# Splitting the LayerNorm and token-mix work of a transformer layer into pairs of chunks between attention steps

## The reference

```python
q = einsum('bsm,hmd->bhsd', x, kernel[0]); k = ... kernel[1]; v = ... kernel[2]
attn = softmax(einsum('bhsd,bhtd->bhst', q, k) / (d * d * h))
out  = einsum('bhst,bhtd->bhsd', attn, v) -> (b, s, d*h);  out = out @ WO[0]
y = layernorm(x + out)
y_prev = y shifted by one token, zero at the start
xr = mu_r * y + (1 - mu_r) * y_prev;  xk = mu_k * y + (1 - mu_k) * y_prev
r = sigmoid(xr @ W_r.T);  k_act = relu(xk @ W_k.T) ** 2
result = layernorm(y + r * (k_act @ W_v.T))
```

## Time and profile before

| what | value |
|---|---|
| median of 3 runs | 2945.0 us (2942.08 to 2955.33) |
| profiled execution | 2821.61 us, span of the slowest core (core 3) 2819.8 us |
| spans of the 8 cores | 2805.7 to 2819.8 us |
| granted TensorE clock, mean | 0.877 to 0.882 |
| TensorE matmul busy | 2124.7 us (75%) |
| ScalarE busy | 1247.8 us (44%) |
| VectorE busy | 835.2 us (30%) |

### The profile page before, as it was taken

How to read it: one execution, slowest core, us unless ns; L and a number is a source line. 1 busy time by engine, 2 the same in 40 slices (tenths; PEclk the granted TensorE clock), 3 DMA queues, 4 the chain that set the end, 5 groups by cost and what they waited for, 6 DMA issues and landing times.

```text
span 2819.8 us, 30056 instructions; the slowest of 8 cores (2805.7 to 2819.8 us)
## 1 busy us (share of the span) xinstructions
PE 2124.7 (75%) x10176; PEld 713.3 (25%) x10176; DVE 835.2 (30%) x1369; ACT 1247.8 (44%) x1441; POOL 20.1 (1%) x27
## 2 busy tenths in 40 slices
PE   0037888778977897789677978887888788878845
PEld 0013322222322232223223322222322222222212
DVE  0012200240434043404362205042233323332365
ACT  0000178357445754574400364646554655365611
POOL 0000000000000000000000000000000000000000
PEclk9998988878988898889888999888988898889867
DMA  9961300000320032002301103000130013001201
GB/s 174 209 169 30 90 1 1 30 1 13 93 90 1 9 96 90 1 4 87 105 15 30 60 30 108 28 30 1 60 105 30 1 60 105 31 1 60 90 30 60
DMA packets 85135, 157.23 MB, mean 56 GB/s; under 512 B 1984, under 2 KB 16384, under 8 KB 84992
## 3 DMA queue, kind: packets, MB, share of 16 engines
q1 hardware_dynamic: 61968, 123.84, 13.5%
q0 software_dynamic: 23024, 31.47, 7.4%
HBM read 155.31 MB, written 31.46 MB: 66 GB/s over the span
## 4 chain that ended last, share of the span: by engine, by line
PE 54%; ACT 18%; DVE 12%; DMA 9%; issue 7%; ACTq 1%; DVEq 0%; POOL 0%; SPq 0%; POOLq 0%
PE psg L99 27%; ACT pb L109 12%; PE pspv L99 10%; PE psden L99 10%; ACT lta L109 4%; DMA ws<-wts 3%; PE psa L99 3%; PE psb L99 3%; DMA wsc<-ws 2%; DVE xka L118 2%; DMA aba<-xT 2%; DVE stv L118 2%; DVE recb L118 2%; DVE xra L118 2%; DVE y L118 2%
## 5 line engine op out<-in xcount | busy, mean ns | idle before, releaser
L109 ACT ACTIVATE pb<-psa 128x1024 bf16<-128x1024 f32 x512 | 522.8, 1021 | 424.5 <-PE psa L99 423.4
L109 ACT ACTIVATE pb<-psb 128x1024 bf16<-128x1024 f32 x512 | 523.8, 1023 | 406.9 <-PE psden L99 230.6
L99 PE MATMUL pspv<-pb,vtb 128*64 128x512 bf16 x2048 | 433.3, 431 | 59.8 <-DVE aba L118 59.7
L99 PE MATMUL psden<-pb,cstb 128*32 128x512 bf16 x2048 | 416.1, 415 | 0.0
L99 PE MATMUL psg<-xra,ws 128*128 128x512 bf16 x1320 | 353.7, 421 | 0.6 <-DVE xra L118 0.6
L99 PE MATMUL psg<-aba,ws 128*128 128x512 bf16 x632 | 164.4, 417 | 241.9 <-DMA ws<-wsc 188.9
L99 PE MATMUL psa<-qtb,ktb 64*128 64x512 bf16 x1024 | 214.2, 409 | 148.6 <-ACT pb L109 88.8
L118 DVE TENSOR_TENSOR aba<-pspv,rsb 128x512 bf16<-128x512 f32 x64 | 44.3, 691 | 814.6 <-ACT rsb L109 814.6
L99 PE MATMUL psb<-qtb,ktb 64*128 64x512 bf16 x1024 | 212.8, 403 | 61.1 <-ACT pb L109 61.1
L99 PEld LDWEIGHTS pspv<-pb,vtb 128*64 128x64 bf16 x2048 | 111.1, 109 | 328.3 <-issue 328.2
L99 PEld LDWEIGHTS psg<-xra,ws 128*128 128x128 bf16 x1320 | 128.3, 105 | 202.2 <-issue 97.2
(11 more groups left out here) (100 smaller groups left out, 1595.0 us busy)
## 6 DMA issues: line engine op xcount, KB each, us to landing
ws<-wsc SPq DMA_DIRECT2D x36, 2048.0 KB, 9.4
ws<-wts POOLq DMA_DIRECT2D x8, 2048.0 KB, 25.3
y<-xT SPq DMA_DIRECT2D x8, 2048.0 KB, 10.4
outT<-outb SPq DMA_DIRECT2D x32, 512.0 KB, 3.5
wsc<-ws SPq DMA_DIRECT2D x7, 2048.0 KB, 13.0
aba<-xT POOLq DMA_DIRECT2D x8, 1024.0 KB, 8.9
xra<-xT POOLq DMA_DIRECT2D x6, 1024.0 KB, 10.0
cstf<-cst SPq DMA_DIRECT2D x1, 96.0 KB, 2.4
```

The lines of the kernel that those rows point to most:

```text
L99: i = e.matmul(_o, _l, _r, start=_st, stop=_sp, tile_position=_tp, skip_group_check=True)
L109: i = e.activation(_o, _i, _f, scale=_s, bias=_b)
```

## The change

The function that broadcasts and applies a LayerNorm is cut into a head (the two `psg<-sr` matmuls and the two activations) and four pieces of one pair of chunks each; the mix is cut into four pieces of one pair each. In the six tiles with `t` > 0 the head becomes a filler of step 19, and application and mix pieces alternate at steps 21, 23, 25, ... 35. LayerNorm 2 of the tile before is cut in the same way: head and four pieces are fillers of their own (due for `t` > 0 at steps 100, 102, ... 108; for `t` = 0 at 75, 77, ... 83). Where a function calls the pieces in a row (the key/value stage and the tail), the order stays as it was.

```diff
-            def emit_ln_bcast_apply(u, dst_y1):
-                Ybuf = OUTB
+            def emit_ln_bcast_head(u, dst_y1):
                 b1 = next_bank()
                 wait("t", c_va, u["nsr"])
...
+            def emit_ln_apply_pair(st, op):
+                if op == 0:
+                    wait("v", c_g, st["nmean"])
+                    wait("v", c_ar, st["nrs"])
+                wait("v", c_va, c_va.n)
...
+                if op == 6:
+                    st["b0b"].free = (c_va, nap)
+                    last_nap[0] = nap
...
+            def emit_mix_pair(u, op):
+                wait("v", c_va, c_va.n)
...
-                        def u_bcast(p=prev):
-                            emit_ln_bcast_apply(p, Y1)[0]
-                            emit_mix(p)
+                        lnst = {}
+                        def u_bhead(p=prev, s=lnst):
+                            s["st"] = emit_ln_bcast_head(p, Y1)
+                        def mk_ap(op, s=lnst):
+                            return lambda: emit_ln_apply_pair(s["st"], op)
+                        def mk_mx(op, p=prev):
+                            return lambda: emit_mix_pair(p, op)
                         fillers.append((17, u_stats))
-                        fillers.append((21, u_bcast))
-                        steps = [50 + 3 * i for i in range(18)]
+                        fillers.append((19, u_bhead))
+                        for i, op in enumerate(range(0, 8, 2)):
+                            fillers.append((21 + 4 * i, mk_ap(op)))
+                            fillers.append((23 + 4 * i, mk_mx(op)))
+                        steps = [50 + 3 * i for i in range(17)]
+                        steps += [100 + 2 * i for i in range(5)]
                     else:
-                        steps = [24 + 3 * i for i in range(18)]
+                        steps = [24 + 3 * i for i in range(17)]
+                        steps += [75 + 2 * i for i in range(5)]
```

More of the change, by code:

```diff
@@ L502, in emit_ln_bcast_apply @@
                 b1.free = (c_ar, nrs)
-                wait("v", c_g, nmean)
-                wait("v", c_ar, nrs)
-                nap = 0
-                naps = []
-                for op in range(0, 8, 2):
[L508 to L524, removed]
@@ L525, in emit_ln_bcast_apply @@
-                b0b.free = (c_va, nap)
-                last_nap[0] = nap
-                return nap, naps
+                return {"b0b": b0b, "nrs": nrs, "nmean": nmean, "naps": [],
+                        "dst": dst_y1}
+            def emit_ln_apply_pair(st, op):
+                Ybuf = OUTB
+                dst_y1 = st["dst"]
+                if op == 0:
+                    wait("v", c_g, st["nmean"])
+                    wait("v", c_ar, st["nrs"])
+                wait("v", c_va, c_va.n)
+                for j, scr in ((op, STV), (op + 1, RECB)):
+                    np1 = vop("scalar_tensor_tensor",
+                              (scr[:, :], st["b0b"].ap[:, :], -1.0,
+                               Ybuf[:, j * QT:(j + 1) * QT],
+                               ALU.mult, ALU.add),
+                              inc=(c_va if j == op + 1 else None))
+                wait("v", c_va, np1)
+                nap = 0
+                for j, scr in ((op, STV), (op + 1, RECB)):
+                    dst = (dst_y1[:, j * 516 + 4: j * 516 + 4 + QT]
+                           if dst_y1 is not None
+                           else Ybuf[:, j * QT:(j + 1) * QT])
+                    nap = vop("tensor_tensor",
+                              (dst, scr[:, :], LTA[:, 512:1024], ALU.mult),
+                              inc=c_va)
+                st["naps"].append(nap)
+                if op == 6:
+                    st["b0b"].free = (c_va, nap)
+                    last_nap[0] = nap
+                return nap
@@ new lines, in emit_ln_bcast_apply @@
+            def emit_ln_bcast_apply(u, dst_y1):
+                st = emit_ln_bcast_head(u, dst_y1)
+                for op in range(0, 8, 2):
+                    emit_ln_apply_pair(st, op)
+                return st["naps"][-1], st["naps"]
+            def emit_mix_pair(u, op):
+                wait("v", c_va, c_va.n)
+                for j, scr in ((op, STV), (op + 1, RECB)):
+                    nd = vop("tensor_tensor",
+                             (scr[:, :], Y1[:, j * 516 + 4: j * 516 + 4 + QT],
+                              Y1[:, j * 516 + 3: j * 516 + 3 + QT],
+                              ALU.subtract),
+                             inc=(c_va if j == op + 1 else None))
+                wait("v", c_va, nd)
+                for j, scr in ((op, STV), (op + 1, RECB)):
+                    vop("scalar_tensor_tensor",
+                        (XRA[:, j * QT:(j + 1) * QT], scr[:, :],
+                         MUS[:, j:j + 1],
+                         Y1[:, j * 516 + 3: j * 516 + 3 + QT],
+                         ALU.mult, ALU.add))
+                for j, scr in ((op, STV), (op + 1, RECB)):
+                    nk = vop("scalar_tensor_tensor",
+                             (XKA[:, j * QT:(j + 1) * QT], scr[:, :],
+                              MUS[:, 8 + j:9 + j],
+                              Y1[:, j * 516 + 3: j * 516 + 3 + QT],
+                              ALU.mult, ALU.add),
+                             inc=(c_va if j == op + 1 else None))
+                wait("v", c_va, nk)
+                if op == 6:
+                    u["mix_done"] = vop(
+                        "tensor_copy",
+                        (bass.AP(Y1, 3, [[NCH * 516, 128], [516, 8], [1, 1]]),
+                         bass.AP(Y1, 515, [[NCH * 516, 128], [516, 8], [1, 1]])),
+                        inc=c_va)
@@ L529, in emit_mix @@
             def emit_mix(u):
-                wait("v", c_va, c_va.n)
                 for op in range(0, 8, 2):
[L532 to L557, removed]
+                    emit_mix_pair(u, op)
             def make_fillers(u, load_wo=True):
@@ L687, in ln2_stats, with ln2_head, ln2_pair, f @@
                     u["nsr"] = nsr
-                def ln2_bcast():
-                    nap, naps = emit_ln_bcast_apply(u, None)
-                    u["naps"] = naps
+                ln2s = {}
+                def ln2_head():
+                    ln2s["st"] = emit_ln_bcast_head(u, None)
+                def ln2_pair(op):
+                    def f():
+                        emit_ln_apply_pair(ln2s["st"], op)
+                        if op == 6:
+                            u["naps"] = ln2s["st"]["naps"]
+                    return f
                 for oc in range(8):
@@ L699, in make_fillers @@
                 fl.append(ln2_stats)
-                fl.append(ln2_bcast)
+                fl.append(ln2_head)
+                for op in range(0, 8, 2):
+                    fl.append(ln2_pair(op))
                 return fl
```

## The result

| | median of runs | undisturbed runs |
|---|---|---|
| changed kernel | 2766.31 us (8 runs) | 2763.74 to 2768.46 |
| kernel before: the three first runs and five timed beside the changed kernel | 2857.57 us (8 runs) | 2817.49 to 2824.43 |

The ratio is 0.9807, with a 95% interval of 0.9794 to 0.9821: on 2821 us, 54.4 us (50.5 to 58.1). I had forecast 54 us. The time forecast, 2891 us with a range of 2866 to 2914, is nevertheless wrong by 125 us, because I took the 54 from 2945. Of either kernel some executions run with a lower TensorE clock on the cores of one die or both and are some per cent longer (one of the changed kernel took 2903.57 us); the others are called undisturbed here. The three runs shown ahead of the prediction (2942 to 2955) are the longest on record of the unchanged kernel, whose undisturbed executions later took 2817 to 2842.

A forecast was written before the change was run, and what follows sets the result against it. TensorE's value matmuls waited 63.4 us for VectorE's multiply, queued behind LayerNorm and mix. Six tiles x (7.1 + 1.7) plus 0.75 gave 54 us off the 2945.0 median: 2891 us, range 2866 to 2914.

The forecast's parts named there:

- the base: Runs' median of 2945.0 us, 123 above the profiled execution; the same 54 us taken off, giving 2891 us.
- First term: Head 1's multiply, six tiles: three pairs' application and mix ahead instead of four, 21.1 us against 28.2; 7.1 us a tile.
- Second term: Statistics matmuls directly behind head 0's epilogue matmul: VectorE starts 1.7 us earlier a tile, ends 0.5 and 3.0.
- What is late next: At head 1, VectorE still last: multiply at +28.1 instead of +36.9, a shorter stop of 2 to 5 us left.
- First rival: Filled hole behind head 0's epilogue keeps clock high: 11 to 13.4 us a tile, 66 to 80, 2872 us; chance 0.17.
- Its second condition: Shorter stop at head 1 shortens low clock behind it from 5 us to 1 or 2, saving 1 to 3 us.
- Second rival: Low-clock stretch around head 1's stop keeps 15 us: 5.2 us a tile left, 2914 us; chance 0.12.
- Slower: Clock does not come back for heads 0 and 1: 9.7 us a tile worse, 3003 us; chance 0.04.
- Edits at nothing: Fourth pair behind multiply, mean's held bank and extra waits cost nothing; the waits bounded by 1 us a tile.

The follow-up runs named there:

- the order alone: Changed kernel with statistics back at step 21, pairs' application and mix given together, three before head 1's multiply, one behind; ratio 0.9837 to the kernel before.
- the version with two pairs: Changed kernel with two pairs' application and mix before head 1's multiply and two behind, instead of three and one; ratio 0.9661 to the kernel before, span 2733.6 us.

## Why the prediction was right in its sum and wrong in its time

**The step that failed: the base.** I wrote that the 123 us between the three runs shown and the profiled execution "is not in the trace", and took the gain from the runs' median. The profiled execution, 2821.61 us, was an undisturbed one. It lies within the 2817.49 to 2824.43 of the undisturbed runs timed beside the changed kernel. From it the forecast is 2768 us, against 2766.31 measured. What made the three first runs 123 us longer stays open, since the clocks of their cores were not recorded. I had both numbers and no evidence for either as the base; a range that covered both bases would have begun near 2740. I gave the base no rival and no chance of its own, though it was more than twice as large as the gain.

**First term, 7.1 us a tile: right.** A pair takes 7.13 us, and the order alone gave 46 us (26 to 65) against 43; the spans differ by 43.

**Second term, 1.7 us a tile with 0.5 and 3.0 as ends: right.** VectorE starts at +5.5 in three tiles and at +7.6 to +8.2 in three; I had +5.7 with the high clock and +8.2 with the low one, and took the middle. The mean place of head 1's multiply is +28.1, as forecast. Alone, this part gave 12 us.

**What is late next: right.** A stop of 2.7 to 4.1 us is left; I had said 2 to 5. From the multiply to head 2's `rsb` it takes 20.9 us in the mean against 21.3, so some 2 us of the gain in six tiles come from there.

**First rival, the clock kept by the filled hole.** It occurred for half of it: in three tiles the scores behind the statistics take 0.39 us, but the second hole is still there. Its 66 us and more were not reached. Its second condition failed: behind the shorter stop the low clock lasts 5 to 6 us in five of six tiles, and not 1 or 2. Adding matmuls in 16 holes gave 16 us in the spans, and taking out the rest of the stop gave about 10 us beyond the stop. By these rows the rule of the Trainium skill ("TensorE: Matmul & The Clock Gate", section "A second HAM failure mode: psum-queue depth-cycling"), that frequent short idles between groups of matmuls cost clock, holds in direction. **Second rival, clock given back:** refuted by the changed kernel itself, in which the low clock ends as soon behind the stop as before and all of the 54 us came, and by the version with two pairs. **Slower:** no sign of it; the mean clocks of the cores were 0.877 to 0.882 and are 0.888 to 0.899.

**Edits at nothing.** The cut of LayerNorm 2 costs nothing that can be told from no change, and the extra waits lengthen a pair from 7.05 to 7.13 us. The held bank costs nothing here and 7 us a tile when four pairs stand behind the multiply.

**Left open.** What decides whether the clock is high or low when head 0's epilogue comes. It is high in three of six tiles of the changed kernel, in four with two pairs, in one with the holes filled as well; in the second profiles of the last two it is three and two. So it differs between two executions of one kernel as well, and the runs do not say by what rule.

## What to carry to other kernels

When an engine that is busy for 30% of the span holds up another, look at what stands in its list ahead of the one instruction that others wait for, and count only the microseconds by which that instruction moves; a stop may shrink or grow without the time following it. Cut long blocks so that as much as possible stands behind that instruction and still ahead of its own user, and check the buffers that the block holds until its end. And before a difference is subtracted, ask of which base: where the profiled execution and the runs shown lie further apart than the expected gain, the base is the largest unknown and needs a chance of its own.

## What the runs showed of the hardware

Work added to an idle hole of TensorE can make a kernel faster. With 22 groups of 8 matmuls whose results nobody reads, the mean granted clocks of the cores went from between 0.896 and 0.907 to between 0.907 and 0.914, and the span fell by 12 us (by 15 in a second pair of profiles). In the changed kernel the hole of 1.75 us behind an epilogue matmul is empty at 23 places, and at 22 of them the scores behind it take 0.61 us (1.2 GHz). Where the hole is filled with the added matmuls they take 0.39 to 0.40 us (2.4 GHz), at all 16 and all 22 places. Filling is not free of the clock: in 3 of the 16 and 5 of the 22 the added group itself ran at the low clock for most of its length and took 3.0 to 3.6 us instead of 1.9.
